# Router logits of a fused FFN kernel with the gate matrix as the stationary operand, in four column tiles

## Chip, cores, metric

One NeuronCore of a Trainium2 chip. The metric is the device time of one execution in microseconds; lower is better.

## What is computed

`x` is (64, 64, 512), 64 batches of 64 channels with 512 features. Each batch picks one of 8 conditioning matrices (64x64) and a bias; after that the 4096 rows of 512 features go through a mixture of 16 experts and one shared expert, and the result is added to `x`:

```python
h = einsum('bct,bcd->bdt', x, w[subjects]) + b[subjects][:, :, None]   # conditioning
h = h.reshape(4096, 512)
logits = h @ gate_weight.T                      # (4096, 16), the part that is changed
scores = sigmoid(logits)
biased = scores + expert_bias
# best 2 of 4 groups of experts by the sum of their top two, then the best 4 experts
w = scores[chosen]; w = w / w.sum() * 2.5
out = sum over the 4 chosen experts of w_e * down_e(silu(gate_e(h)) * up_e(h))
out = out + shared_down(silu(shared_gate(h)) * shared_up(h))
return x + out
```

All arrays are fp32.

## The kernel before

The rows are cut into 32 tiles of 128 (NT = 32). The kernel has a **first stage** (one loop over n = 0 to 33, written out), then the FFN of 32 tiles through the shared expert, then the FFN of 143 tiles of rows sorted by expert. Every engine has its own program; they meet by semaphores. Nothing plans the order but the order of the statements.

The first stage is a pipeline over the tiles. In iteration n

- **TensorE (PE)** multiplies tile n by its conditioning matrix (L770, `psY`, one fp32 product with 512 moving columns), transposes tile n-1 in four 128x128 blocks (L745, `psT`) and makes the logits of tile n-2 (L787, `psGU`): four products, one for each 128 features, with the transposed tile (128x128) stationary and the gate's 16 columns moving. It waits for tile n-2's evacuation before L770, for tile n-1's before the transposes, and for the copy of the transposed tile before the logits. An fp32 product shows as two weight loads and two matmuls in the trace, a transpose as one of each. After iterations 18 and 26 PE makes position sums for the routing (L755, L756; `PE_POS`).
- **ScalarE (ACT)** evacuates tile n with its bias to `tok_ring` (L625), copies the transposed tile n-1 to `kept_w` or, for the last eight, `x_ring` (L629), and takes the sigmoid of the logits of tile n-2 (L632). After iterations 16, 19 and 22 it also makes a third of the shared expert's split weights (L606).
- **GpSimd (POOL)** copies two 64x64 conditioning matrices into `cw_ring` for tile n (L537), up to eight tiles ahead of PE. After tile 4's it makes the late constants (`late_consts`, L493 and L501), after tile 10's it issues the DMAs that clear the padding rows.
- **SyncE (SP)** issues the load of tile n+8 when L770 has used tile n (L388), at n = 8 the load of the shared expert's weights (L395), and the store of tile n (L397). ACT waits for the store of tile n-8 before it overwrites its slot of `tok_ring`.
- **VectorE (DVE)** routes a batch of eight tiles when `scored` says that their sigmoids are there (`route_groups` and what follows). Batches 0 to 2 belong to this stage, and batch 1 is followed by three splits of shared weights (L1252). After batch 2 DVE makes the split of the first FFN tile (L1269), which PE's first FFN product waits for.

The FFN loop (PE L837, transposes L745) follows in the same programs. There PE carries in some iterations small products for the tables: L799 with a stationary operand of one column and 143 moving columns in fp32, L863 with 128x128 fp16 stationary and 144 moving.

Of the kernel before, what the change touches and what calls it, by code (L numbers as in the profile page):

```python
# [11 lines left out]
ACT = mybir.ActivationFunctionType  # L12
AX = mybir.AxisListType

P = 128
B, C, H = 64, 64, 512
N = B * C
NT = N // P
E, TOPK = 16, 4
# [3 lines left out]
HK, IK = H // P, I // P  # L23
UP = HK * 2 * I
EW = UP + IK * H
BC = 8
# [12 lines left out]
Q = P // QUADS  # L39
# [36 lines left out]
LOWS = {21: ((1, 0),), 23: ((1, 1),), 24: ((1, 2),), 26: ((2, 0),), 29: ((2, 1),), 31: ((2, 2),)}  # L76
RAW_LOADS = {14: 1, 15: 2, 23: 3, 31: 4}
WARM_UP = 12
X_COPIES = {1: 1, 5: 2, 9: 3, 13: 4, 17: 5, 21: 6, 25: 7}
FIRST_X_COPY = 30  # L80
WEIGHTS_STORE = 3
# [17 lines left out]

def tile_at(n):  # L100
    return Tile(n // RING, n % RING)


def run_tiles(eng, first, head, rounds, tail, step):
# [14 lines left out]
def build(nc, x, itok, fside, cond_w, gate_w, expert_bias, ffn_w, out):  # L119
# [4 lines left out]
    with ExitStack() as ctx:  # L124
        def sb(name, shape, dt=F32):
            return ctx.enter_context(nc.sbuf_tensor(name, shape, dt))

        def ps(name):
            return ctx.enter_context(nc.psum_tensor(name, [P, 512], F32))

        def sem(name):
            return ctx.enter_context(nc.semaphore(name))


        ident = sb("ident", [P, P])
# [14 lines left out]
        subj1h = sb("subj1h", [NS, B])  # L150
        fside2 = sb("fside2", [NS, 2 * C])
        bias_tok = sb("bias_tok", [P, NT])
        gate_sb = sb("gate_sb", [P, HK * E])
        ebias = sb("ebias", [P, E])
        raw_w = sb("raw_w", [P, 2 * EW])
        with nc.sbuf_tensor("kept_w", [P, SPLITS * 2 * EW], F32) as kept_w:
# [20 lines left out]
        scores = sb("scores", [P, NT * E])  # L177
# [93 lines left out]
        psY = [ps(f"psY{i}") for i in range(2)]  # L271
        psH = ps("psH")
        psM = ps("psM")


        consts = sem("consts")
# [23 lines left out]
        a_xposed = sem("a_xposed")  # L300
        a_xT_ready = sem("a_xT_ready")
        logits_done = sem("logits_done")
        scored = sem("scored")
        dve = sem("dve")
        cum_ready = sem("cum_ready")
# [57 lines left out]
        def kept_xT(tile):  # L363

            if tile >= NT - KEPT_IN_X:
                return x_ring[:, tile % RING, :]
            at = (1 + tile // KEPT) * 2 * EW + KEPT_ORDER[tile % KEPT] * H
            return kept_w[:, at:at + H]
# [220 lines left out]
        def _(act):  # L589
# [28 lines left out]
            for n in range(NT + 2):  # L618
                t = tile_at(n)
                if n < NT:  # L620
                    act.wait_ge(cond_done, n + 1)
                    if n >= RING:
                        act.wait_ge(h_stored[t.slot], t.rnd * 16)
                        act.wait_ge(a_xposed, n + 1 - RING)
                    act.activation(tok_ring[:, t.slot, 0:H], psY[n % 2][:], ACT.Identity,  # L625
                                   bias=bias_tok[:, n:n + 1]).then_inc(h_ready, 1)
                if 1 <= n <= NT:
                    act.wait_ge(a_xposed, n)
                    act.activation(kept_xT(n - 1), psT[(n + 1) % 2][:], ACT.Copy).then_inc(a_xT_ready, 1)  # L629
                if n >= 2:  # L630
                    act.wait_ge(logits_done, n - 1)
                    act.activation(scores[:, (n - 2) * E:(n - 1) * E], psGU[n % 2][:, 0:E],  # L632
                                   ACT.Sigmoid).then_inc(scored, 1)
                if n in SHARED_HIGH:
                    if SHARED_HIGH[n] == 0:
                        act.wait_ge(shared_loaded, 16)
                    split_high(0, SHARED_HIGH[n])
                elif n == FIRST_X_COPY:
                    copy_x(0)
                if n in (NT - 2, NT - 1):  # L640
                    copy_xT(tile_at(n - (NT - 2)), n - (NT - 2))
# [50 lines left out]
            def step(t, n, j):  # L692
# [19 lines left out]
                elif n in HIGHS:  # L712
# [4 lines left out]
                    split_high(turn, j)  # L717
                if n in X_COPIES:
                    copy_x(X_COPIES[n])

# [7 lines left out]
        def _(pe):  # L728
            pe.wait_ge(blank, 2)
            for _ in range(WARM_UP):  # L730
                pe.matmul(psM[:, 0:P], ones[:], ones[:], start=True, stop=True)  # L731
# [16 lines left out]
            def positions(b):  # L748
# [10 lines left out]
                    mm = pe.matmul(psM[:, BE:BE + E], ones[:], cum[:, NT, :], start=True, stop=True)  # L759
                mm.then_inc(pos_done, 1)  # L760

            for n in range(NT + 2):
                t = tile_at(n)
                if n < NT:

                    pe.wait_ge(x_in[t.slot], (t.rnd + 1) * 16)
                    pe.wait_ge(cond_w_ready, 2 * (n + 1))
                    if n >= 2:
                        pe.wait_ge(h_ready, n - 1)
                    pe.matmul(psY[n % 2][:], cw_ring[:, t.slot, :], x_ring[:, t.slot, :],  # L770
                              start=True, stop=True).then_inc(cond_done, 1)
                if n == 0:
                    bias()
                elif n == 2:
                    pe.wait_ge(small_loaded, SMALL)
                if 1 <= n <= NT:
                    pe.wait_ge(h_ready, n)
                    if n >= 3:
                        pe.wait_ge(a_xT_ready, n - 2)
                    transposes(psT[(n - 1) % 2], tok_ring[:, (n - 1) % RING, 0:H], HK).then_inc(a_xposed, 1)  # L780
                if n >= 2:
                    pe.wait_ge(a_xT_ready, n - 1)
                    if n >= 4:
                        pe.wait_ge(scored, n - 3)
                    xT = kept_xT(n - 2)
                    for k in range(HK):
                        mm = pe.matmul(psGU[n % 2][:, 0:E], xT[:, k * P:(k + 1) * P],  # L787
                                       gate_sb[:, k * E:(k + 1) * E], start=(k == 0), stop=(k == HK - 1))
                    mm.then_inc(logits_done, 1)
                if n in PE_POS:  # L790
                    positions(PE_POS[n])
# [73 lines left out]
                                   skip_group_check=True)  # L865
                mm.then_inc(table_done, 1)

            pe.wait_ge(scored, NT - 1)
            pe.wait_ge(h_ready, NT)
            pe.wait_ge(low_done, PIECES)  # L870
            kept = []
# [1 line left out]
            def step(t, n, j):  # L873
                if j == 0:
                    kept.clear()
                if n == NT:
                    pe.wait_ge(words_ready, 1)
                elif n == 1:
                    pe.wait_ge(scored, NT)
                at, needed = weights(t, n)  # L880
                kept.append(at)
                gate_up(t, n, kept[-1], needed)
                if n != 0:
                    xpose_hid(t + -1, None if n is None else n - 1)
                if n in PE_POS_FFN:
                    positions(PE_POS_FFN[n])
                elif n == PE_WORDS:
                    word_tables()
                elif n == PE_SP_WORDS:
                    sp_table()  # L890
                if is_shared(n):
                    for g in ENTRY_STEPS.get(n - 1, ()):
                        fill_slots(g)
                if n is None or n >= 2:
                    down(t + -2, None if n is None else n - 2,
                         kept[-3] if j >= 2 else weights(t + -2, None if n is None else n - 2)[0])
# [7 lines left out]
        def _(v):  # L904
# [43 lines left out]
            for half in range(2):  # L948
                a, b = half * C, half * C + C
# [16 lines left out]

            def route_groups(b):

                v.wait_ge(scored, (b + 1) * BC)
                tt(per_chunk(masked[:], E), per_chunk(batch(scores, b), E), over_chunks(ebias[:], BC), ALU.add)  # L970
                settle()
                four = masked[:].rearrange("p (g j) -> p g j", j=GS)
                tt(pair_sums[:, :, 0:3], four[:, :, 0:3], four[:, :, 1:4], ALU.add)
                tt(pair_sums[:, :, 3:5], four[:, :, 0:2], four[:, :, 2:4], ALU.add)
                tt(pair_sums[:, :, 5:6], four[:, :, 0:1], four[:, :, 3:4], ALU.add)
                settle()
                put(v.tensor_reduce(group_sum[:], pair_sums[:], AX.X, ALU.max))
                settle()

                sums = per_chunk(group_sum[:], NG)  # L980
                for d in range(1, NG):
                    last = d + (NG + 1) * (NG - 1 - d)
                    tt(beats[:, :, d:last + 1:NG + 1], sums[:, :, d:NG], sums[:, :, 0:NG - d], ALU.is_gt)
                settle()
                put(v.tensor_reduce(group_up[:], beats[:].rearrange("p c (a b) -> p c a b", b=NG), AX.X, ALU.add))
                put(v.tensor_reduce(group_down[:], beats[:].rearrange("p c (a b) -> p c b a", b=NG), AX.X, ALU.add))
                settle()
                tt(group_down[:], group_down[:], group_c[:], ALU.add)
                settle()
                tt(group_up[:], group_up[:], group_down[:], ALU.is_ge)  # L990
                settle()
                stt(four, spread(group_up[:].rearrange("p c g -> p (c g)"), GS), -BIG, four, ALU.mult, ALU.add)
                settle()
# [63 lines left out]
            used, not_last, start, end, turn, prep, prep_end = [e_rows[:, k, :] for k in range(7)]  # L1057
# [393 lines left out]
```

## Time and profile before

| | |
|---|---|
| median of 3 runs | 873.62 us (869.86 to 874.09) |
| the profiled execution's own time | 872.52 us |
| its span, first to last instruction | 870.8 us |
| PE busy | 851.7 us (98%) |
| DVE / ACT / POOL busy | 484.6 / 421.2 / 440.2 us |
| first stage, until the first L837 on the chain of waits | 79.74 us |

The span leaves 1.7 us of the profiled execution outside it. Times in the rows are microseconds from the span's start unless they are marked ns. PE is the matmul side of TensorE and PEld its weight loads; a matmul's duration includes its way through the array, so that matmuls one behind the other overlap in the timeline, and the chain of waits shows the time that each really adds. A line number can be that of a helper.

### The profile page before, as it was taken

What the parts mean: (1) busy time and instruction counts of PE and PEld (TensorE: products, weight loads), DVE (VectorE), ACT (ScalarE), POOL (GpSimd) and SP (SyncE); (2) the same over time, 40 slices, a digit from 0 to 9 for tenths busy, and PEclk for the clock granted to TensorE, in tenths of its full rate; (3) what the DMA queues carried; (4) which work ended last, traced back from release to release, by engine and by line L of the source; (5) the groups of instructions that cost most, each with busy time, mean ns of one, the idle gap of its engine ahead of it and who ended that gap; (6) DMA issues with size and microseconds to landing.
All of it is one profiled execution on the core that took longest, in us unless ns stands there. A gap on an engine that the chain in (4) does not pass through costs nothing.

```text
span 870.8 us, 19587 instructions
## 1 busy us (share of the span) xinstructions
PE 851.7 (98%) x4144; PEld 691.9 (79%) x4145; DVE 484.6 (56%) x1055; ACT 421.2 (48%) x884; POOL 440.2 (51%) x402
## 2 busy tenths in 40 slices
PE   9999999999999999999999999999999999999994
PEld 7778887878888888878888888888787878887883
DVE  1467786564654444664446645756557456464440
ACT  4675345754544444544445544645445455353441
POOL 4330211125547555656656666655655575755333
PEclk9999999999999999999999999999999999999998
DMA  8974576659999999999988999899798999989644
GB/s 258 352 277 145 114 128 164 165 110 291 258 219 270 195 183 188 176 221 281 209 179 172 234 260 226 176 269 229 193 280 178 284 243 234 244 179 194 123 62 62
DMA packets 147097, 179.10 MB, mean 206 GB/s; under 512 B 30986, under 2 KB 104210, under 8 KB 144658
## 3 DMA queue, kind: packets, MB, share of 16 engines
q0 software_dynamic: 37296, 86.95, 50.0%
q1 hardware_dynamic: 108258, 80.41, 35.1%
q10 hardware_dynamic: 1408, 10.49, 3.6%
q14 instruction: 117, 0.96, 0.4%
q8 instruction: 18, 0.29, 0.2%
HBM read 82.48 MB, written 65.04 MB: 169 GB/s over the span
## 4 chain that ended last, share of the span: by engine, by line
PE 85%; issue 4%; DVE 2%; ACT 2%; DMA 2%; SPq 1%; POOL 1%; DVEq 1%; ACTq 0%
PE psGU L837 48%; PE psY L837 24%; PE psH L745 4%; PE psY L770 3%; PE psGU L787 3%; DMA out<-y_ring,idx_all 2%; PE psT L745 2%; POOL out L553 1%; SPq L418 1%; ACT x_ring L689 1%; DVE entry L1244 1%; PE psM L731 1%; DVE x_ring L1246 1%; ACT y_ring L656 0%; ACT xT_hi L616 0%
## 5 line engine op out<-in xcount | busy, mean ns | idle before, releaser
L837 PE MATMUL psGU<-split_w,xT_hi 128*128 (+1 forms) x1400 | 432.6, 390 | 5.0 <-issue 2.7
L553 POOL DMA_INDIRECT out<-y_ring,idx_all x143 | 233.6, 1634 | 208.2 <-SPq L457 187.0
L837 PEld LDWEIGHTS psGU<-split_w,xT_hi 128*128 128x128 f32 x1400 | 261.9, 188 | 63.7 <-issue 8.1
L837 PE MATMUL psGU<-split_w,xT_lo 128*128 (+1 forms) x700 | 273.4, 391 | 0.0
L837 PE MATMUL psY<-split_w,hidT_hi 128*128 (+1 forms) x700 | 232.6, 413 | 0.2 <-issue 0.2
L704 ACT ACTIVATE aT<-psGU 128x256 f32<-128x256 f32 x175 | 67.2, 384 | 256.0 <-PE psGU L837 204.3
L1269 DVE TENSOR_TENSOR xT_lo<-psT,xT_hi 128x512 fp32r<-128x512 f32 x143 | 98.8, 691 | 150.6 <-ACT xT_hi L616 92.1
L548 POOL DMA_INDIRECT tok_ring<-h_rows,idx_all x143 | 150.2, 1051 | 57.6 <-issue 42.6
L656 ACT ACTIVATE y_ring<-psY 128x512 f32<-128x512 f32 x175 | 103.7, 593 | 127.3 <-PE psY L837 90.2
L837 PEld LDWEIGHTS psGU<-split_w,xT_lo 128*128 128x128 f32 x700 | 131.4, 188 | 27.4
L837 PE MATMUL psY<-split_w,hidT_lo 128*128 (+1 forms) x350 | 137.6, 393 | 0.0
L837 PEld LDWEIGHTS psY<-split_w,hidT_hi 128*128 128x128 f32 x700 | 118.5, 189 | 16.5 <-issue 0.7
L1294 DVE SCALAR_TENSOR_TENSOR aT<-aT,w_ring,psGU 128x256 f32<-128x256 f32 x143 | 66.9, 468 | 86.8 <-ACT aT L704 57.5
L1276 DVE STREAM_TRANSPOSE psT<-x_ring 128x512 f32<-128x512 f32 x143 | 102.5, 717 | 0.0
L561 POOL DMA_DIRECT2D out<-y_ring x32 | 28.4, 900 | 122.9 <-ACT y_ring L656 122.7
L616 ACT ACTIVATE xT_hi<-psT 128x512 fp32r<-128x512 f32 x143 | 84.7, 592 | 1.7 <-DVE psT L1276 1.2
L837 PEld LDWEIGHTS psY<-split_w,hidT_lo 128*128 128x128 f32 x350 | 65.7, 188 | 14.4
L1282 DVE TENSOR_TENSOR hidT_lo<-psH,hidT_hi 128x256 fp32r<-128x256 f32 x175 | 72.8, 416 | 2.1 <-ACT hidT_hi L647 1.3
L1309 DVE TENSOR_TENSOR split_w<-raw_w,split_w x42 | 51.5, 1226 | 39.1 <-ACT split_w L666 21.6
L647 ACT ACTIVATE hidT_hi<-psH 128x256 fp32r<-128x256 f32 x175 | 66.4, 380 | 3.0 <-PE psH L745 3.0
L745 PEld LDWEIGHTS psH<-ident,aT 128*128 128x128 f32 x350 | 48.7, 140 | 24.1 <-DVE aT L1292 1.3
L745 PE MATMUL psH<-ident,aT 128*128 128x128 f32 x350 | 66.6, 271 | 0.5 <-DVE hidT_lo L1282 0.5
(178 smaller groups left out, 495.7 us busy)
## 6 DMA issues: line engine op xcount, KB each, us to landing
x_ring<-tok_ring SPq DMA_DIRECT2D x284, 128.0 KB
raw_w<-ffn_w SPq DMA_DIRECT2D x17, 1536.0 KB, 10.4
h_rows<-tok_ring SPq DMA_DIRECT2D x32, 256.0 KB, 3.9
out<-y_ring POOLq DMA_DIRECT2D x32, 256.0 KB
x_ring<-x SPq DMA_DIRECT2D x24, 256.0 KB, 4.3
tok_ring<-h_rows,idx_all POOLq DMA_INDIRECT x143
out<-y_ring,idx_all POOLq DMA_INDIRECT x143
x_ring<-x ACTq DMA_DIRECT2D x8, 256.0 KB, 3.6
```

What stands on the lines that cost most here:

```text
L548: pool.indirect_dma_start(tok_ring[:, r % RING, :], None, h_rows[:, :], bass.IndirectOffsetOnAxis(idx_all[:, r:r + 1], 0)).then_inc(gather ...
L553: pool.indirect_dma_start(out[:, :], bass.IndirectOffsetOnAxis(idx_all[:, r:r + 1], 0), y_ring[:, r % YRING, :], None, compute_op=ALU.add) ...
L616: act.activation(xT_hi[:, t.slot % 2, :], xT, ACT.Copy).then_inc(xhi_ready, 1)
L647: act.activation(hidT_hi[:, t.slot % 2, :], psH[:, 0:I], ACT.Copy).then_inc(hidhi_ready, 1)
L656: act.activation(y_ring[:, s, :], psY[t.slot % 2][:], ACT.Copy).then_inc(y_ready, 1)
L704: act.activation(silu[:, t.slot % 2, :], psGU[t.slot % 2][:, 0:I], ACT.Silu).then_inc(silu_ready, 1)
L745: mm = pe.transpose(dst[:, k * P:(k + 1) * P], src[:, k * P:(k + 1) * P], ident[:])
L837: mm = pe.matmul(dst, a[:, slot, c], w(at + col + k * H), start=(k == 0 and a is high and at == 0), stop=(k == parts - 1 and a is low))
L1269: v.tensor_tensor(xT_lo[:, t.slot % 2, :], xT, xT_hi[:, t.slot % 2, :].bitcast(F32), ALU.subtract).then_inc(xT_ready, 1)
L1276: v.transpose(psT[t.slot % 2][:].rearrange("p (k b j) -> p k j b", k=HK, j=QUADS), x_duo[:, t.slot // DUO_TILES, :, t.slot % DUO_TILES, :] ...
L1282: v.tensor_tensor(hidT_lo[:, t.slot % 2, :], psH[:, 0:I], hidT_hi[:, t.slot % 2, :].bitcast(F32), ALU.subtract).then_inc(hidT_ready, 1)
L1294: ins = v.scalar_tensor_tensor(out=hid[:, half, :], in0=gate, scalar=w_ring[:, w_slot, bass.ds(expert, 1)], in1=up, op0=ALU.mult, op1=ALU. ...
```

## The change

The logits of tiles 0 to 27 are made in seven groups of four tiles. The gate matrix is padded from 16 to 32 columns and is now the stationary operand (128x32), the transposed tile (128x128) the moving one, and tile j of a group goes to the column tile j of TensorE (`tile_position=(0, j * Q)`), that is to partitions 32j to 32j+31 of `psLT`. That gives logits with the experts on partitions and the rows on the free axis. ACT copies the 128x128 block to SBUF (`logitsT`), PE turns it by one transpose (`psL`), and ACT takes one sigmoid of 128x64 for four tiles. Group g is made in iteration 4g+5 and turned in iteration 4g+6. Tiles 28 to 31 keep the former way, in iterations 30 to 33. Both PSUM blocks are columns 256 to 511 of `psH`. `scored` now counts 7 groups and then 4 tiles, and all who wait for it are changed to match.

```diff
@@ -76,6 +76,9 @@
 LOWS = {21: ((1, 0),), 23: ((1, 1),), 24: ((1, 2),), 26: ((2, 0),), 29: ((2, 1),), 31: ((2, 2),)}
 RAW_LOADS = {14: 1, 15: 2, 23: 3, 31: 4}
 WARM_UP = 12
+LOGIT_TILES = P // Q
+LOGIT_GROUPS = NT // LOGIT_TILES - 1
+DIRECT = LOGIT_GROUPS * LOGIT_TILES
 X_COPIES = {1: 1, 5: 2, 9: 3, 13: 4, 17: 5, 21: 6, 25: 7}
 FIRST_X_COPY = 30
 WEIGHTS_STORE = 3
@@ -99,6 +102,13 @@
 
 def tile_at(n):
     return Tile(n // RING, n % RING)
+
+
+def scored_by(tiles):
+
+    if tiles <= DIRECT:
+        return tiles // LOGIT_TILES
+    return LOGIT_GROUPS + tiles - DIRECT
 
 
 def run_tiles(eng, first, head, rounds, tail, step):
@@ -150,7 +160,8 @@
         subj1h = sb("subj1h", [NS, B])
         fside2 = sb("fside2", [NS, 2 * C])
         bias_tok = sb("bias_tok", [P, NT])
-        gate_sb = sb("gate_sb", [P, HK * E])
+        gate_sb = sb("gate_sb", [P, HK * Q])
+        logitsT = sb("logitsT", [P, P])
         ebias = sb("ebias", [P, E])
         raw_w = sb("raw_w", [P, 2 * EW])
         with nc.sbuf_tensor("kept_w", [P, SPLITS * 2 * EW], F32) as kept_w:
@@ -271,6 +282,7 @@
         psY = [ps(f"psY{i}") for i in range(2)]
         psH = ps("psH")
         psM = ps("psM")
+        psLT, psL = psH[:, 2 * P:3 * P], psH[:, 3 * P:4 * P]
 
 
         consts = sem("consts")
@@ -300,6 +312,8 @@
         a_xposed = sem("a_xposed")
         a_xT_ready = sem("a_xT_ready")
         logits_done = sem("logits_done")
+        logitsT_ready = sem("logitsT_ready")
+        logits_turned = sem("logits_turned")
         scored = sem("scored")
         dve = sem("dve")
         cum_ready = sem("cum_ready")
@@ -627,8 +641,17 @@
                 if 1 <= n <= NT:
                     act.wait_ge(a_xposed, n)
                     act.activation(kept_xT(n - 1), psT[(n + 1) % 2][:], ACT.Copy).then_inc(a_xT_ready, 1)
-                if n >= 2:
-                    act.wait_ge(logits_done, n - 1)
+                g, phase = divmod(n - LOGIT_TILES, LOGIT_TILES)
+                if 0 <= g < LOGIT_GROUPS and phase == 1:
+                    act.wait_ge(logits_done, g + 1)
+                    act.activation(logitsT[:], psLT, ACT.Copy).then_inc(logitsT_ready, 1)
+                elif 0 <= g < LOGIT_GROUPS and phase == 2:
+                    act.wait_ge(logits_turned, g + 1)
+                    act.activation(scores[:, g * LOGIT_TILES * E:(g + 1) * LOGIT_TILES * E].rearrange(
+                        "p (j e) -> p j e", e=E), psL.rearrange("p (j q) -> p j q", q=Q)[:, :, 0:E],
+                        ACT.Sigmoid).then_inc(scored, 1)
+                if n - 2 >= DIRECT:
+                    act.wait_ge(logits_done, scored_by(n - 1))
                     act.activation(scores[:, (n - 2) * E:(n - 1) * E], psGU[n % 2][:, 0:E],
                                    ACT.Sigmoid).then_inc(scored, 1)
                 if n in SHARED_HIGH:
@@ -759,6 +782,25 @@
                     mm = pe.matmul(psM[:, BE:BE + E], ones[:], cum[:, NT, :], start=True, stop=True)
                 mm.then_inc(pos_done, 1)
 
+            def group_logits(g):
+
+                pe.wait_ge(a_xT_ready, (g + 1) * LOGIT_TILES)
+                if g > 0:
+                    pe.wait_ge(logitsT_ready, g)
+                for k in range(HK):
+                    for j in range(LOGIT_TILES):
+                        mm = pe.matmul(psLT[j * Q:(j + 1) * Q, :], gate_sb[:, k * Q:(k + 1) * Q],
+                                       kept_xT(g * LOGIT_TILES + j)[:, k * P:(k + 1) * P],
+                                       start=(k == 0), stop=(k == HK - 1), tile_position=(0, j * Q))
+                mm.then_inc(logits_done, 1)
+
+            def turn_logits(g):
+
+                pe.wait_ge(logitsT_ready, g + 1)
+                if g > 0:
+                    pe.wait_ge(scored, g)
+                pe.transpose(psL, logitsT[:], ident[:]).then_inc(logits_turned, 1)
+
             for n in range(NT + 2):
                 t = tile_at(n)
                 if n < NT:
@@ -778,14 +820,19 @@
                     if n >= 3:
                         pe.wait_ge(a_xT_ready, n - 2)
                     transposes(psT[(n - 1) % 2], tok_ring[:, (n - 1) % RING, 0:H], HK).then_inc(a_xposed, 1)
-                if n >= 2:
+                g, phase = divmod(n - LOGIT_TILES, LOGIT_TILES)
+                if 0 <= g < LOGIT_GROUPS and phase == 1:
+                    group_logits(g)
+                elif 0 <= g < LOGIT_GROUPS and phase == 2:
+                    turn_logits(g)
+                if n - 2 >= DIRECT:
                     pe.wait_ge(a_xT_ready, n - 1)
-                    if n >= 4:
-                        pe.wait_ge(scored, n - 3)
+                    if n - 4 >= DIRECT:
+                        pe.wait_ge(scored, scored_by(n - 3))
                     xT = kept_xT(n - 2)
                     for k in range(HK):
                         mm = pe.matmul(psGU[n % 2][:, 0:E], xT[:, k * P:(k + 1) * P],
-                                       gate_sb[:, k * E:(k + 1) * E], start=(k == 0), stop=(k == HK - 1))
+                                       gate_sb[:, k * Q:k * Q + E], start=(k == 0), stop=(k == HK - 1))
                     mm.then_inc(logits_done, 1)
                 if n in PE_POS:
                     positions(PE_POS[n])
@@ -865,7 +912,7 @@
                                    skip_group_check=True)
                 mm.then_inc(table_done, 1)
 
-            pe.wait_ge(scored, NT - 1)
+            pe.wait_ge(scored, scored_by(NT - 1))
             pe.wait_ge(h_ready, NT)
             pe.wait_ge(low_done, PIECES)
             kept = []
@@ -876,7 +923,7 @@
                 if n == NT:
                     pe.wait_ge(words_ready, 1)
                 elif n == 1:
-                    pe.wait_ge(scored, NT)
+                    pe.wait_ge(scored, scored_by(NT))
                 at, needed = weights(t, n)
                 kept.append(at)
                 gate_up(t, n, kept[-1], needed)
@@ -966,7 +1013,7 @@
 
             def route_groups(b):
 
-                v.wait_ge(scored, (b + 1) * BC)
+                v.wait_ge(scored, scored_by((b + 1) * BC))
                 tt(per_chunk(masked[:], E), per_chunk(batch(scores, b), E), over_chunks(ebias[:], BC), ALU.add)
                 settle()
                 four = masked[:].rearrange("p (g j) -> p g j", j=GS)
@@ -1436,7 +1483,8 @@
         "itok": np.ascontiguousarray(itok_B_0_7),
         "fside": np.tile(np.asarray(fside_8xS_0), (1, 2)),
         "cond_w": np.tile(np.asarray(L0_cond_weights).transpose(1, 0, 2).reshape(C, NS * C), (2, 1)),
-        "gate_w": np.ascontiguousarray(columns(np.asarray(L0_ffn_gate_weight)[None])[0].reshape(P, HK * E)),
+        "gate_w": np.ascontiguousarray(np.pad(columns(np.asarray(L0_ffn_gate_weight)[None])[0],
+                                              ((0, 0), (0, 0), (0, Q - E))).reshape(P, HK * Q)),
         "expert_bias": np.ascontiguousarray(L0_ffn_expert_bias),
         "ffn_w": np.ascontiguousarray(ffn_w),
     }
```

## Rows read from the trace of the kernel before

**Rows 1.** The page: the chain that ended last, by engine and by line

```profile
PE 85%; issue 4%; DVE 2%; ACT 2%; DMA 2%; SPq 1%; POOL 1%; DVEq 1%; ACTq 0%
PE psGU L837 48%; PE psY L837 24%; PE psH L745 4%; PE psY L770 3%; PE psGU L787 3%; DMA out<-y_ring,idx_all 2%; PE psT L745 2%; POOL out L553 1%; SPq L418 1%; ACT x_ring L689 1%; DVE entry L1244 1%; PE psM L731 1%; DVE x_ring L1246 1%; ACT 
```

**Rows 2.** Windows of the first stage: PE, PEld, DVE, ACT, POOL busy (x), clock, DMA share, GB/s

```profile
40.00:60.00 20.00, 20.00 (x131) 15.39 (x130) 12.76 (x46) 14.71 (x30) 9.09 (x28) 1.00 0.93 327
60.00:80.00 20.00, 19.99 (x137) 15.99 (x136) 10.44 (x46) 12.65 (x30) 0.04 (x1) 1.00 0.46 164
```

**Rows 3.** The chain in order of time, first stage: start us, us, what

```profile
16.41 0.72 issue
17.13 1.10 PE psY L770 x2
...
39.18 0.95 PE psY L770 x2
40.13 0.44 PE psT L745 x4
40.57 0.80 PE psGU L787 x8
...
47.95 0.32 PE psM L755 x2
48.26 0.22 PE psM L756 x2
48.48 0.86 PE psY L770 x2
...
79.74 5.57 PE psGU L837 x24
```

**Rows 4.** Groups of PE and PEld instructions, 0 to 86 us, shapes apart

```profile
L787 PE MATMUL psGU<-gate_sb,kept_w 128*128 128x16 f32 x192 | 23.1, 253 | 0.0
L787 PEld LDWEIGHTS psGU<-gate_sb,kept_w 128*128 128x128 f32 x192 | 23.3, 192 | 0.0
```

**Rows 5.** The chain in order of time, two stretches of the FFN: start us, us, what

```profile
124.47 0.52 PE psM L863 x8
...
138.61 2.08 PE psT L799 x18
```

**Rows 6.** Timeline of ACT in iteration 16: start, us

```profile
42.36 0.69 ACT L625 ACTIVATE tok_ring<-psY,bias_tok 128x512 f32<-128x512 f32 x1 [0.77 <-PE psY L770]
42.95 0.59 ACT L629 ACTIVATE kept_w<-psT 128x512 f32<-128x512 f32 x1
43.60 0.18 ACT L632 ACTIVATE scores<-psGU 128x16 f32<-128x16 f32 x1
43.68 1.05 ACT L606 ACTIVATE split_w<-raw_w 128x1024 fp32r<-128x1024 f32 x1
```

**Rows 7.** Timeline of POOL: start, us; the copies for tiles 5, 16 and 17

```profile
16.51 0.52 POOL L537 COPY cw_ring<-cond_sb 64x64 f32 x2 [1.90 <-issue]
...
35.62 0.57 POOL L537 COPY cw_ring<-cond_sb 64x64 f32 x2 [2.42 <-issue]
38.75 0.53 POOL L537 COPY cw_ring<-cond_sb 64x64 f32 x2 [2.57 <-PE psY L770]
```

**Rows 8.** DMA: windows of 2 us, columns as in rows 2

```profile
42.00:44.00 2.00, 2.00 (x15) 1.60 (x14) 0.00 (x0) 1.57 (x4) 0.46 (x2) 1.00 1.06 403
...
54.00:56.00 2.00, 2.00 (x15) 1.47 (x14) 1.76 (x8) 1.17 (x4) 1.04 (x4) 1.00 0.77 210
```

**Rows 9.** DMA: issue to landing of the loads of x at L388

```profile
DMA to landing us min/median/max: 2.6/4.3/12.3
```

**Rows 10.** Timeline of DVE: routing of batch 2 and the first FFN tile's split

```profile
63.98 0.29 DVE L920 TENSOR_TENSOR masked<-scores,ebias 128x128 f32<-128x128 f32 x1 [4.32 <-ACT scores L632]
...
73.69 0.23 DVE L1049 TENSOR_SCALAR weights_te<-w_num 128x128 f32<-128x128 f32 x1
76.52 0.69 DVE L1269 TENSOR_TENSOR xT_lo<-x_ring,xT_hi 128x512 fp32r<-128x512 f32 x1 [2.60 <-ACT xT_hi L616]
```

## The prediction

> **What bounds the kernel now.** I read the page's chain first: PE's work makes 85% of it, and the lines of the first stage stand in it, L770 with 3% and the logits, L787, with 3% [rows 1]. Windows of that stage show PE busy throughout at a granted clock of 1.00, its full level (2.4 GHz), ACT, the nearest other engine, at 14.7 of 20 us at most, but the DMA engines at a share of 0.93 from 40 to 60 us [rows 2]. The chain in order of time shows one iteration: 0.95 us for the conditioning product, 0.44 for four transposes, 0.80 for the logits, 2.19 together, nothing between them [rows 3]. So time taken from PE in this stage shortens the kernel until another wait comes up; the nearest are looked at below. The logits' 256 weight loads and matmuls (192 of each in the first form) stream 16 columns, and a pair adds 0.80/8 = 0.10 us though the matmul lasts 253 ns and the load 192 [rows 3, 4]: they pay for loading 128 columns.
>
> One stretch gives nothing. In iteration 5 PE waits 0.72 us until 17.13 us for the conditioning matrix of tile 5 [rows 3], which POOL copies only at 16.51, behind the late constants [rows 7]. The logits of tiles 0 to 2 lie ahead of that; without them PE only waits longer.
>
> **The change, part by part.**
>
> *Removed:* the logits of tiles 3 to 27, which lie behind 17.13 us: 25 x 0.80 = 20.0 us [rows 3].
>
> *A weight load uncovered before, covered after:* L770 adds 0.95 us behind logits but 0.86 behind the position sums, which stream 128 columns [rows 3]. Of the 26 iterations 6 to 31, seven stay behind a group, one behind direct logits and two were behind position sums already, so 16 x 0.09 = 1.4 us go.
>
> *Added, seven groups of logits.* A group is 16 fp32 products (four blocks of features, four tiles), each two passes: 32 loads and 32 matmuls of 128 fp32 moving columns. Such a pass costs 0.44/4 = 0.11 us in the transposes [rows 3], and with a small stationary operand 2.08/18 = 0.116 for 143 columns [rows 5], by columns 0.104; I take 0.107. Whether passes in different columns of the array overlap, no row shows. The bounds are 32 x 0.107 = 3.4 us, one behind the other, and 8 x 0.107 = 0.86, all four column tiles at once. I take the middle: the code issues both passes of a product together, and both need the same column tile, so the second has to follow the first; if PE starts matmuls in program order, only the second pass of one product runs beside the first of the next. That is 16 x 0.107 = 1.71 us. The issue of instructions allows it: eight fp16 pairs add 0.52 us, 0.065 a pair [rows 5], and 32 x 0.065 = 2.1 is thus an upper bound for issue alone.
>
> "TensorEngine Tiling (Array Packing)" of the Trainium skill (Theoretical Speedup) gives up to 4x for 32 columns; by it a group would be 0.86 us. "TensorE: Matmul & The Clock Gate" of the Trainium skill (Part 3) says that matmuls start and end in program order; by it 1.71 stands. No row here decides between them.
>
> *Into and out of the column tiles:* if the array must empty first, each change costs what a matmul outlasts its addition, 0.253 - 0.10 = 0.15 us [rows 3, 4]; if not, nothing. I take the whole, 0.32 us a group with the two rounded up, since the other end is only hoped for. (The Trainium skill, "TensorEngine Tiling (Array Packing)", Key Properties, says that a change of tiling mode drains TensorE.)
>
> *Seven transposes:* 0.11 us each. Together 7 x (1.71 + 0.32 + 0.11) = 15.0 us.
>
> *ACT.* An iteration takes it 0.59 + 0.65 = 1.24 us (starts 42.36, 42.95, 43.60) [rows 6] against 0.86 + 0.44 = 1.30 on PE in those without a group. Per four tiles, four sigmoids of 0.18 give way to a copy of 128 columns and a sigmoid of 64; their cost lies between 0.18 and 0.59 each by the same rows, some 0.5 us together. The 1.05 us of L606 [rows 6] had 0.95 us of slack each iteration (2.19 - 1.24); now after iterations 19 and 22 a transpose waits for the late evacuation, about 0.5 us each; after 16 the group of iteration 17 covers it. I add 1.0 us. The waits for the copy and the turned block have an iteration of other work between them, and what is queued behind them on ACT, the next tile's evacuation, isn't due before; nothing for them.
>
> *POOL, DMA, DVE.* Four tiles then take 4 x 1.30 + 0.09 + 2.14 = 7.4 us. Tile 17's product comes at 17.13 + 3 x 7.4 = 39.4 us, where POOL's copy for it, not held by PE for all that row's name says (tile 9 had passed), ends at 39.3 [rows 7]: just enough. The load of x for eight tiles later has 14.9 - 0.9 = 14.0 us, and landing took at most 12.3 [rows 9]. The DMA engines moved 403 GB/s while saturated and 210 by 54 us when a backlog (shared weights, cleared padding) was gone [rows 8]; 0.52 MB for each 1.86 us is 282 GB/s, so the backlog still drains, later. The gate's 32 KB more go nowhere near a wait. Batch 2's routing takes from 63.98 to 73.92 us, 9.9 us, and the FFN begins 15.8 us after its start [rows 3, 10]; after, its scores come in iteration 26, some 13 us ahead of the FFN. The first split then starts in time. Nothing for all of these. The FFN behind starts earlier with all its work and passes the gain on.
>
> **Sum:** -20.0 - 1.4 + 15.0 + 1.0 = -5.4 us. The profiled execution took 872.5 us and would take 867.1; it lies 1.1 us under the median, so the median goes from 873.6 to **868.2 us**.
>
> **The rivals.**
>
> *All four column tiles at once* (chance 0.21). For it: loads and matmuls of one product already overlap [rows 4]. Then 7 x (0.86 + 0.32 + 0.11) = 9.0 us and a sum of -11.4. But tile 17 would be due at 17.13 + 12 x 1.30 + 0.27 + 3 x 1.29 = 36.9 us, 2.4 us before POOL has it [rows 7], and the lead of a load of x falls to 12.3 us, what the longest needed [rows 9]. So -9.0: 864.6 us.
>
> *No overlap, and TensorE loses* (0.22). The 32 passes stand one behind the other: 7 x (3.42 + 0.32 + 0.11) = 27.0 us against 21.4 taken away, ACT's stalls gone with the slower pace: +5.6, 879.2 us. It decides from 2.63 us a group upward, (21.4/7) less 0.43. For it: no row shows two matmuls side by side at more than the array's rate; against: a column tile leaves three quarters of the array free.
>
> *The gain is taken by the next wait* (0.12): the pairs overlap, but POOL's 2.5 us gaps [rows 7], which came at a DMA share of 1, grow with a longer backlog, or the splits of ACT hold more than I count. Three to five us go: about 872 us.
>
> The forecast has the remaining 0.45, its own range -4 to -7.5 us by the drain paid or not.
>
> **How the numbers follow.** About 0.5%, 4.4 us, is what a measurement of this kernel can tell from no change. The forecast lies just beyond it, two thirds of its chance above: 0.31 faster, 0.14 same. Full overlap is faster. No overlap is slower by more than that if the drain is paid (0.15), else same (0.07). The third rival is same. Faster 0.52, same 0.33, slower 0.15. The range from 862.5 to 878.5 takes in full overlap with part of POOL's wait and cuts off the worse half of no overlap.
>
> **What would show it.** The chain of waits would have seven pieces of 32 matmuls on `psH`; by the forecast each adds 1.7 to 2.1 us, by full overlap about 1.0, by none 3.4 or more. L770 would add 0.86 us in most iterations. The first FFN product would start at 74.3 us in place of 79.74. ACT would have gaps behind PE of about half a microsecond near its splits, POOL none that PE waits for after tile 5. The forecast is wrong if the groups' pieces are near either end, if PE waits for POOL or a load of x in iterations 12 to 20, or if an earlier start of the FFN isn't seen at the end. A granted clock under 1.00 in the stage would upset every term.

## The result, and the profile after

The changed kernel took **864.07 us** (median of 6 runs, 861.59 to 866.22) against 873.48 us (6 runs, 869.86 to 875.10) for the kernel before: a ratio of 0.989, 95% interval 0.9868 to 0.9913, so 9.4 us less. Run again beside other kernels it took 864.10 us against 872.34, ratio 0.9913 (0.9884 to 0.9942). The forecast was 868.2 us, 5.4 less, in a range of 862.5 to 878.5.

| profiled execution | before | after |
|---|---|---|
| its own time | 872.52 us | 861.59 us |
| span | 870.8 us | 859.8 us |
| PE busy | 851.7 us | 838.1 us |
| first stage, until the first FFN product on the chain | 79.74 us | 72.25 us |
| the rest of the span | 791.1 us | 787.5 us |

The chain that ended last in the changed kernel, by line; it answers to [rows 1] (L884 is L837 of before, L812 is L770, L834 the direct logits of L787, L792 the new groups):

```profile
PE psGU L884 52%; PE psY L884 26%; PE psH L768 4%; PE psY L812 3%; PE psT L768 1%; DMA x_ring<-x 1%; PE psH L792 1%; ACT x_ring L712 1%; DVE entry L1291 1%; DVE x_ring L1293 1%; POOL out L567 1%; ACT split_w L620 0%; PE psGU L834 0%; ACT xT
```

The logits' 3% are gone down to 1% for L792 and less for L834, and a new piece stands there, a load of x. The chain in order of time, in the changed kernel, which answers to [rows 3] (start us, us, what):

```profile
13.94 3.66 issue
17.60 2.05 PE psY L812 x2
19.65 0.85 PE psT L768 x4
20.50 1.87 PE psH L792 x32
22.37 1.73 PE psY L812 x2
...
28.54 1.01 PE psH L792 x32
29.55 1.05 PE psY L812 x2
...
31.04 0.11 PE psH L802
...
32.05 9.33 DMA x_ring<-x
...
41.43 1.12 PE psY L812 x2
...
49.70 0.66 PE psT L768 x4
...
72.25 5.60 PE psGU L884 x24
```

A group of 32 matmuls adds **1.01 us** (28.54), which is full overlap and not pairs. Its turning transpose adds 0.11 (31.04). The product behind a group adds 1.05 us, 0.19 over the 0.86 of a covered load. But the first group adds 1.87 us, and the pieces beside it are long too: PE waited 3.66 us for tile 5's matrix (13.94), and after that its clock was at half. The windows of 2 us show it (PE, PEld, DVE, ACT, POOL busy (x), granted clock, DMA share, GB/s):

```profile
14.00:16.00 2.00, 0.00 (x0) 0.00 (x0) 0.00 (x0) 0.71 (x2) 0.85 (x1) 1.00 1.04 383
16.00:18.00 2.00, 0.40 (x1) 0.43 (x2) 0.00 (x0) 0.00 (x0) 0.47 (x2) 0.72 0.82 309
18.00:20.00 2.00, 2.00 (x5) 0.86 (x5) 0.00 (x0) 0.31 (x1) 0.93 (x4) 0.50 0.10 37
...
22.00:24.00 2.00, 2.00 (x11) 0.80 (x4) 0.00 (x0) 0.28 (x1) 1.33 (x3) 0.58 0.17 56
24.00:26.00 2.00, 2.00 (x13) 1.44 (x12) 0.00 (x0) 1.75 (x4) 2.00 (x4) 1.00 0.75 192
```

No matmul ran from 14 to 16 us; from 16 to 24 us the granted clock falls to 0.50, the lower of its two levels (1.2 GHz), and back to 1.00 (2.4 GHz) in the window from 24. The four pieces from 17.60 us take 2.05 + 0.85 + 1.87 + 1.73 = 6.50 us; at the full level, by the same chain and [rows 3], they are 1.10 + 0.44 + 1.01 + 1.05 = 3.60. So in this trace the wait, of which 0.72 us was there before [rows 3], costs 2.9 us more through the clock.

Who kept PE waiting in the stage, changed kernel, 10 to 74 us (us in total, times, longest us):

```profile
PE psY L812 <- issue: 3.7, 1, 3.7
PE psY L812 <- DMA x_ring<-x: 1.2, 1, 1.2
PE psT L768 <- ACT tok_ring L639: 0.4, 2, 0.2
```

The first line is the wait for POOL's copies for tile 5, which began at 16.98 us and took 0.52, the second the load of x for tile 17, in iteration 17 (texts below that were written before a run call it iteration 13, a miscount of mine), the third ACT held by the splits. Per load of x, issue to landing went from a median of 4.3 us to 7.8, at a longest of 10.4 (12.3 before, [rows 9]):

```profile
DMA to landing us min/median/max: 2.5/7.8/10.4
```

The load that PE waits for took 9.3 us on the chain, from its issue at 32.05 us. Tile 9's product, which frees its slot, had ended at 28.1 us. SP's timeline around it (start us, us):

```profile
27.80 1.24 SPq L402 DMA_DIRECT2D x_ring<-x  x1
29.09 1.55 SPq L409 DMA_DIRECT2D raw_w<-ffn_w  x1
30.68 1.33 SPq L411 DMA_DIRECT2D h_rows<-tok_ring  x1
32.05 0.89 SPq L402 DMA_DIRECT2D x_ring<-x  x1
```

The issues of tile 16's load, of the shared weights and of a store stand ahead of it in SP's program and take 1.24, 1.55 and 1.33 us, at a DMA share of 1.0. So the load was asked for 4.0 us after its slot was free, took 9.3 us more, and was needed sooner than before, since the iterations were shorter.

### The profile page after: what moved, and what is told of

The parts are those of the page before. It is cut to its first block, busy times and chain, and to the rows that moved or that the text cites. A ratio compares the mean times of both kernels' runs of the same rounds, so it can differ in the third digit from the quotient of the medians.

```text
span 859.8 us, 19571 instructions
## 1 busy us (share of the span) xinstructions
PE 838.1 (97%) x4151; PEld 675.4 (79%) x4152; DVE 485.0 (56%) x1055; ACT 418.1 (49%) x870; POOL 439.2 (51%) x402
## 4 chain that ended last, share of the span: by engine, by line
PE 89%; issue 3%; ACT 3%; DVE 2%; DMA 1%; POOL 1%; DVEq 0%; ACTq 0%; SPq 0%
PE psGU L884 52%; PE psY L884 26%; PE psH L768 4%; PE psY L812 3%; PE psT L768 1%; DMA x_ring<-x 1%; PE psH L792 1%; ACT x_ring L712 1%; DVE entry L1291 1%; DVE x_ring L1293 1%; POOL out L567 1%; ACT split_w L620 0%; PE psGU L834 0%; ACT xT_hi L630 0%; PE psM L910 0%
## 5 line engine op out<-in xcount | busy, mean ns | idle before, releaser
L884 PE MATMUL psGU<-split_w,xT_hi 128*128 (+1 forms) x1400 | 432.0, 390 | 3.0 <-DVE xT_lo L1316 3.0
L884 PEld LDWEIGHTS psGU<-split_w,xT_hi 128*128 128x128 f32 x1400 | 262.2, 188 | 60.2 <-issue 4.2
L884 PE MATMUL psGU<-split_w,xT_lo 128*128 (+1 forms) x700 | 273.4, 391 | 0.0
L884 PE MATMUL psY<-split_w,hidT_hi 128*128 (+1 forms) x700 | 232.5, 413 | 0.2 <-issue 0.2
L562 POOL DMA_INDIRECT tok_ring<-h_rows,idx_all x143 | 148.2, 1037 | 61.0 <-issue 42.7
L884 PEld LDWEIGHTS psGU<-split_w,xT_lo 128*128 128x128 f32 x700 | 131.4, 188 | 27.4
L884 PE MATMUL psY<-split_w,hidT_lo 128*128 (+1 forms) x350 | 137.5, 393 | 0.0
L884 PEld LDWEIGHTS psY<-split_w,hidT_hi 128*128 128x128 f32 x700 | 118.5, 189 | 16.1 <-issue 0.5
L884 PEld LDWEIGHTS psY<-split_w,hidT_lo 128*128 128x128 f32 x350 | 65.7, 188 | 14.4
```

Of the source, the lines that this page charges most:

```text
L562: pool.indirect_dma_start(tok_ring[:, r % RING, :], None, h_rows[:, :], bass.IndirectOffsetOnAxis(idx_all[:, r:r + 1], 0)).then_inc(gather ...
L884: mm = pe.matmul(dst, a[:, slot, c], w(at + col + k * H), start=(k == 0 and a is high and at == 0), stop=(k == parts - 1 and a is low))
```

## Experiments

**Is it four column tiles side by side, or cheap passes?** Two runs. `j_outer` exchanges the loops of a group, so that eight passes in one column tile follow one another:

```diff
-                for k in range(HK):
-                    for j in range(LOGIT_TILES):
+                for j in range(LOGIT_TILES):
+                    for k in range(HK):
```

> The changed kernel with the two loops of a group exchanged, so that the eight passes of one tile, all in one column tile, stand one behind the other. Theory A (column tiles work side by side, passes in the same column tile one behind the other): a group's piece on the chain goes from 1.01 us to 3.4 us (32 x 0.107), or a little less where the last pass of one tile overlaps the first of the next, and the FFN starts 7 x 2.3 = 16 us later. Rival B (a narrow stationary operand alone makes a pass of 128 columns cost 0.03 us, wherever it goes): the piece stays at 1.0 us and the start of the FFN stays within 1 us.

`one_tile` leaves out three of four tiles' logits in groups 1 to 6:

```diff
-                    for j in range(LOGIT_TILES):
+                    for j in range(LOGIT_TILES if g == 0 else 1):
```

> The changed kernel with groups 1 to 6 making the logits of their first tile only (8 of 32 passes; the logits of the other three tiles are left over from group 0). Theory A (four column tiles fully side by side): the eight passes in one column tile take as long as the 32 in four, 8 x 0.107 = 0.86 us and 0.15 on the way in, so a group's piece stays at 1.01 us. Rival B (each pass costs 0.03 us wherever it goes): 0.25 to 0.4 us a piece. Forecast on record (pairs of passes side by side) would have had 0.86 against 1.71.

The chains in order of time, first `j_outer`, then `one_tile`:

```profile
26.67 2.39 PE psH L792 x32
```

```profile
28.08 0.99 PE psH L792 x8
```

Eight passes in one column tile take 0.99 us, as long as the 32 in four (1.01): the column tiles run fully side by side, and rival B is out (it wanted 0.4 at most). With the loops exchanged the same 32 passes take 2.39 us, so the order matters; but it is 2.39 and not 3.4. The FFN accordingly starts 5.3 us later than in the changed kernel (77.53 against 72.25 us; 71.58 in `one_tile`) and not 16: the groups add 7 x 1.38 = 9.7 us, and the half clock (2.9) and the wait for x (1.5 with the longer piece behind it) are absent from this trace. How many matmuls are in flight shows why. Windows of 0.05 us over a group, L792 alone (x counts the matmuls and loads that run in the window), changed kernel:

```profile
28.45:28.50 0.05, 0.03 (x4) 0.04 (x6) 1.00 0.50 205
28.55:28.60 0.05, 0.05 (x5) 0.05 (x8) 1.00 0.64 248
28.60:28.65 0.05, 0.05 (x8) 0.05 (x8) 1.00 0.34 123
28.70:28.75 0.05, 0.05 (x12) 0.05 (x8) 1.00 1.26 497
28.75:28.80 0.05, 0.05 (x12) 0.05 (x4) 1.00 1.06 412
```

The same for `one_tile`, and then for `j_outer`:

```profile
28.35:28.40 0.05, 0.05 (x3) 0.05 (x2) 1.00 1.02 410
```

```profile
26.95:27.00 0.05, 0.05 (x3) 0.05 (x1) 1.00 1.03 420
27.05:27.10 0.05, 0.05 (x4) 0.05 (x4) 1.00 0.95 376
27.30:27.35 0.05, 0.05 (x6) 0.05 (x3) 1.00 0.45 164
28.00:28.05 0.05, 0.05 (x6) 0.05 (x3) 1.00 1.31 532
```

One column tile has 3 matmuls in flight, each 0.27 us long and 0.11 apart. The changed kernel has 12, four times as many: four start in the first 0.05 us, the next four 0.13 us after the first, and the others at steps of 0.11. In `j_outer` there are 3 at first and then 5 or 6, two column tiles' worth: the second tile's first passes start 0.46 us into the group, when not more than five of the first tile's eight have started. Starts in strict program order would have held them back until 0.75 us and given 3 x 0.75 + 0.99 = 3.2 us in all. So by these figures PE looks past matmuls that wait for their column tile, but not far enough for more than two tiles at eight passes each; the order that spreads neighbours over the tiles gets all four. When the next tile begins in `j_outer`, three passes of the tile before it are still waiting; in the changed kernel the fourth tile's first pass would go past three waiting second passes, if the instructions stand as in the code. One reach, of three waiting matmuls, would fit both orders; no run tried it. (The Trainium skill, "TensorE: Matmul & The Clock Gate", Part 3, says that matmuls start and end in program order; `j_outer` does not agree, unless the passes of different products stand in another order in the instructions than in the code, which no view here shows.) `j_outer` lasted 871.28 us in its one run, 871.16 the median of before; one run can't show the 2.2 us by which its FFN starts ahead of 79.74.

**What do the wait for POOL and the half clock cost?** `kept_warm` fills the wait with work that leaves its result unused:

```diff
+                elif n == 4:
+                    for _ in range(WARM_UP + 4):
+                        pe.matmul(psM[:, 0:P], ones[:], ones[:], start=True, stop=True)
```

> The changed kernel with 16 more fp32 products of ones with ones, 128 columns, on PE at the end of iteration 4, in the time in which it waits for the conditioning matrix of tile 5 (32 passes x 0.107 = 3.4 us of a wait of 3.66). Theory: the granted clock stays at 1.00, the product of tile 5 still starts at about 17.6 us, but the pieces of iterations 5 and 6 that took 2.05, 0.85, 1.87 and 1.73 us take 1.1, 0.44, 1.0 and 1.05, so that the FFN starts 2.9 us earlier (69.3 us instead of 72.25) unless the wait for a load of x in iteration 13, 1.2 us, grows by as much. Rival (PE only runs into the loads of x sooner, the lost clock costs nothing): the wait in iterations 12 to 15 grows to about 4 us and the FFN starts at 71.5 to 72.3. Total 861 by the theory, 864 by the rival.

The clock stayed at 1.00 throughout the stage; `kept_warm`, windows of 2 us:

```profile
16.00:18.00 2.00, 2.00 (x15) 1.64 (x15) 0.00 (x0) 0.53 (x1) 0.70 (x3) 1.00 0.62 240
18.00:20.00 2.00, 2.00 (x39) 1.36 (x37) 0.00 (x0) 1.29 (x4) 0.92 (x4) 1.00 0.33 68
20.00:22.00 2.00, 2.00 (x9) 1.13 (x9) 0.00 (x0) 1.25 (x3) 0.87 (x5) 1.00 0.59 220
```

The first two groups added 1.01 us each. But the FFN started at 71.05 us, 1.2 earlier and not 2.9: between the theory's 69.3 and the rival's 71.5. In `kept_warm` PE waits for a load of x until 40.22 us, 1.75 us, and before that for POOL in iterations 12 and 13:

```profile
29.48 1.10 PE L812 MATMUL psY<-x_ring,cw_ring 128*128 128x512 f32 x2 [0.19 <-issue]
31.62 1.10 PE L812 MATMUL psY<-x_ring,cw_ring 128*128 128x512 f32 x2 [0.60 <-issue]
40.22 1.12 PE L812 MATMUL psY<-x_ring,cw_ring 128*128 128x512 f32 x2 [1.75 <-DMA x_ring<-x]
```

Both accounts are half right: the clock's 2.9 us are real, and POOL and the loads take 1.7 of them back. The total, 865.98 us against 871.16 (ratio 0.9933, 0.9904 to 0.9962), does not show even the 1.2; it is above the 861 and 864 us that were expected, and the measurement does not tell it from the changed kernel's 0.989.

`tables8` moves the cause of the wait, POOL's late constants, behind tile 8 (`PAIR_TABLES = 8` for 4):

> The changed kernel with POOL's late constants behind the copies for tile 8 instead of tile 4. Theory: PE does not wait for POOL after tile 4 and the clock stays up; the 3.66 us of waiting and 2.9 us of half clock go, unless DMA takes them back: the loads of x for tiles 8 to 15 are asked for earlier, but the DMA engines are at a share of about 1. With all of it the FFN starts at 65.7 us; I expect 2 to 3 us of waits for loads of x to stay or come, so 67 to 69 us and a total of 859 to 861. Rival (DMA is what sets the pace of the stage after tile 8): the start stays above 71 us.

The FFN started at 71.65 us: the rival's side. The wait was only moved, to tile 9, and took the clock with it (1.6 us by the pieces behind it); and shorter ones for POOL came up behind it, 2.3 us together. `tables8`, chain in order of time:

```profile
20.55 2.41 issue
22.95 1.11 PE psY L812 x2
...
24.92 1.87 PE psH L792 x32
...
31.70 0.96 issue
...
38.63 0.81 issue
```

So the time behind tile 8 was POOL's and the DMA engines' to give, and the next runs go there. (Total 860.99 us against 871.16, ratio 0.9864, 0.982 to 0.9908: as low as expected, though the start of the FFN was not.)

**Who holds POOL's copies and the loads of x?** `pads31` issues the four DMAs that clear the padding rows, 2.1 MB, after tile 31 (`PAD_STORES = 31` for 10):

> The changed kernel with the four DMAs that clear the padding rows issued by POOL after tile 31's copies instead of tile 10's. In the traces so far POOL's copies for a tile come 1.0 to 1.3 us apart before those DMAs and about 2 us apart for some eight tiles behind them, and the wait for tile 13's load of x ends at 41 us, when the DMA engines have been at a share of 1 for 14 us. Theory (these DMAs hold up both): the copies stay 1.0 to 1.3 us apart, the 1.2 us wait for x in iteration 13 goes, and the FFN starts at 70.5 to 71.0 us, with the half clock of iterations 5 and 6 still there. Rival (the shared weights and the tiles' own traffic saturate the DMA engines): the wait for x stays over 0.8 us and the start within 0.4 us of 72.25.

The wait for x went, and the FFN started at 70.48 us, at the lower edge of the theory's, with the half clock still there. The longest landing of a load of x fell to 9.2 us:

```profile
DMA to landing us min/median/max: 2.5/6.7/9.2
```

The issue of tile 17's load came 1.0 us after tile 9's product had ended (27.8 us) and not 4.0, because the issues ahead of it on SP took 0.43 us each:

```profile
28.78 0.43 SPq L402 DMA_DIRECT2D x_ring<-x  x1
```

POOL's copies stayed 1.0 to 1.7 us apart until 34 us, but then went to 1.2 to 2.4 without those DMAs, when the DMA engines were still at a share of 1. So in this one trace the wait for x went with the padding, which explains only the first part of POOL's slow copies; what slows the rest was not settled. Total 861.54 us against 872.19, ratio 0.9872 (0.983 to 0.9915).

`t12_p31` adds `PAIR_TABLES = 12`:

> As pads31, and POOL's late constants behind the copies for tile 12 instead of tile 4. Theory: PE waits for POOL nowhere, the clock stays at 1.00, all of the 3.66 + 2.9 + 1.4 us of waits and half clock goes: FFN start at 64.5 to 66 us, total 6 to 7 us under the changed kernel. Rival (waits for loads of x take at least half of it back, since eight tiles of x are in flight and now asked for earlier): start at 68 to 70 us.

FFN start at 66.49 us, just behind the theory's window: the half clock of the stage is gone, of the waits for POOL one of 1.68 us is left, now in iteration 13, and one of 0.3. `t12_p31`, chain in order of time:

```profile
26.72 1.68 issue
...
35.41 0.29 issue
```

The total, 860.49 us (ratio 0.9847, 0.9797 to 0.9898), is 3.6 us under the changed kernel's and not 6 to 7: the part behind the stage took 793.1 us, 5.6 more than in the changed kernel's trace. Of these the last section has a reason for 1.6.

`t12_p31_splits` adds the move of ACT's split pieces:

```diff
-SHARED_HIGH = {16: 0, 19: 1, 22: 2}
+SHARED_HIGH = {17: 0, 21: 1, 25: 2}
```

> As t12_p31, and ACT's three pieces of the shared weights' split after iterations 17, 21 and 25, in which PE has a group, instead of 16, 19 and 22. Theory: PE's two waits for an evacuation held up by them, 0.5 us each, go; FFN start 1.0 us before that of t12_p31. Rival (ACT is then late for the group's copy and the next evacuation): no difference within 0.3 us, the waits only move.

FFN start at 65.29 us, 1.2 earlier. The product of tile 18, which stands ahead of the waits behind the splits, already started 0.4 us earlier, with 1.4 us of waits for POOL in place of 2.0; the other 0.8 are the two waits for ACT. The chain has no piece of ACT between 15 and 64 us any more. The theory holds: a split in an iteration with a group costs nothing. The totals, 860.49 and 859.86 us, don't tell the two apart.

`before_t12_p31` makes the same two moves on POOL in the kernel before:

> The kernel before with the same two moves on POOL (late constants behind tile 12, clearing DMAs behind tile 31). Theory: there only the wait of 0.72 us for tile 5's matrix exists, so the FFN starts at 79.0 us instead of 79.74 and the total is the same within what can be measured. If the total falls by more than 2 us, the moves are worth something by themselves and not only with the change.

FFN start at 78.71 us, 870.0 us against 872.19, ratio 0.9975 (0.9948 to 1.0003). The moves are worth one microsecond of stage there, 5.8 in the changed kernel (72.25 to 66.49), by one trace of each; two traces of the changed kernel differ by 1.1 (below). Before, other work of PE covered most of what they take away: PE waited once, for 0.72 us, and not at all in `before_t12_p31`.

**All together.** `combined` is `t12_p31_splits` with the two fp16 tables of the late constants also made after tile 31 (DVE's wait for them moves to where it uses them), and `after_again` the changed kernel beside it:

```diff
+            def fp16_consts():
                 iota(lane_q[:], [[1, P], [0, DUO]], 0, 0)
...
                 elif n == PAD_STORES:
                     clear_pads()
+                    pool.wait_ge(cond_w_ready, 2 * (n + 1))
+                    fp16_consts()
```

> As t12_p31_splits, and the two fp16 tables, 3.2 us of the late constants, made by POOL after tile 31 with the clearing DMAs; the other constants stay behind tile 12. Theory: the last wait of PE for POOL, 1.36 us in iteration 13, goes: FFN start at 63.5 to 64.2 us, 1.3 us before t12_p31_splits, and the total 4 to 6 us under after_again. Rival (POOL's slow copies, not the constants, make that wait, or a load of x takes its place): start at 65 us or later.

> The changed kernel itself, unaltered, beside the next run on the same chip: it gives what its FFN start and its FFN part vary by. FFN start again at 71.5 to 73 us with half clock after tile 5's wait; the rest of the span between 787 and 793 us, as in the ten traces so far.

`combined` took **854.52 us** (853.22 to 862.03) against 864.10 for `after_again` and 872.34 for the kernel before; its ratio to the latter is 0.981 (0.9775 to 0.9845), apart from the changed kernel's 0.9884 to 0.9942. Its FFN starts at 63.30 us, a bit ahead of the theory's window, and the total is 9.6 us under `after_again`, more than the 4 to 6 expected. The profile lists no wait of PE in the stage, while for `after_again` it lists these (10 to 74 us):

```profile
PE psY L812 <- issue: 3.2, 1, 3.2
PE psY L812 <- DMA x_ring<-x: 2.5, 1, 2.5
```

The DMA engines of `combined` are busier than before [rows 2], and PE waits for nobody (windows as above):

```profile
20.00:40.00 20.00, 20.00 (x177) 12.56 (x176) 10.47 (x50) 16.15 (x32) 8.18 (x34) 1.00 1.02 364
40.00:60.00 20.00, 20.00 (x184) 13.09 (x182) 18.53 (x77) 16.56 (x33) 11.96 (x21) 1.00 0.96 349
```

`after_again` started its FFN at 73.34 us, a microsecond beyond the changed kernel's first trace (outside what I expected by 0.3), with a wait for x of 2.5 us instead of 1.2, after which the clock was at half a second time.

## Why the prediction came out as it did

The total lay in the range and on the forecast side, but that is in part luck. The step that carried the sum failed: the seven groups cost 8.5 us and not 15.0, and costs that the sum did not have (the half clock 2.9, a load of x 1.5, tile 5's later matrix 0.5) took 4.9 of the difference back. By the signs that it named itself it was wrong: the groups' pieces lie at the end that full overlap gave, PE waited for a load of x in iteration 17, and the granted clock fell under 1.00. The stage gave 7.5 us in the first trace (6.4 in `after_again`), the medians of the total 9.4 (8.2); where the rest comes from was not settled.

- *What bounds it:* right. Time taken from PE in the stage shortened the kernel. Over the twelve traces, with FFN starts from 63.3 to 79.7 us, the rest of the span was 787.4 to 793.5 us. The three earliest starts have 793.0 to 793.5, for 1.6 us of which the last section has a reason in two of them; but `kept_warm`, with a start at 71.05, has 792.8 too, so whether an early start costs the FFN something was not settled. Of the first trace's 11.0 us, 7.5 are the stage's, and the other 3.5 lie within that spread.
- *Tiles 0 to 2 give nothing:* right, and worse. The 0.72 us wait grew to 3.66, as was said; that such a wait can take the clock down was not said. It cost 2.9 us in the first trace, and `kept_warm` shows that work in the wait keeps the clock up.
- *The group, 1.71 us, by pairs of passes:* **this step failed**. It is 1.01 us, 0.86 for eight times four passes side by side and 0.15 on the way in. The forecast's premise, that the second pass of a product holds up the next product, is refuted by the 12 matmuls in flight, with four starts in 0.05 us; it would have been nearer in `j_outer`, where 2.39 us were measured. The rival with all four tiles at once (chance 0.21) had the mechanism, and by it 864.6 us, half a microsecond from the measured 864.1, but not by its own reason: it took 2.4 us off for POOL's copy of tile 17, and what came off was the clock and a load of x. Its stage sum was -9.0 against -7.5, so that its total came so near is luck too.
- *Into and out of the column tiles, 0.32 us:* it measured 0.15 on the way in and 0.19 on the product behind, 0.34, where 0.09 of the latter was counted in the line before. The size is right. The drain that the Trainium skill ("TensorEngine Tiling (Array Packing)", Key Properties) states fits these rows, though they don't tell it from a weight load that can't be made ahead.
- *A covered load of L770 saves 0.09:* right, 0.86 us in every iteration without a group before it, outside the waits.
- *ACT, 1.0 us:* right. The two waits behind the splits cost 0.42 us each (0.20 of idleness and 0.22 of a longer piece of transposes, 0.66 in place of 0.44), 0.8 together, and `t12_p31_splits` takes them away.
- *POOL just enough, DMA lead 14.0 us:* POOL was in time after tile 5, since the half clock had given it 2.9 us. The lead of a load was not: four iterations took 6.5 us and not 7.4, which leaves 13.0 - 0.9 = 12.1 us, and 4 of them went by before SP issued the load. That cost 1.2 us of wait and 0.26 of a longer piece. The forecast counted the time to landing and not the time to issue.

With the measured terms the sum is -20.0 - 1.4 + 7 x (1.01 + 0.10 + 0.11) + 2.9 (clock) + 1.5 (x) + 0.8 (ACT) + 0.5 (tile 5's matrix came that much later) - 0.2 (the two position sums add 0.22 us behind a transpose and added 0.32 behind logits) = -7.4 us, against -7.5 on the chain.

## To carry to other kernels

Small products with a stationary side of 32 columns are worth putting in column tiles, if the loop changes the tile with every product: the same 32 passes took 1.01 us so and 2.39 in the other order. The swap of the operands alone would have gained nothing: by `one_tile` four tiles in one column tile are estimated at 4 x 0.86 = 3.4 us, against 4 x 0.80 = 3.2 for the direct logits. When work is taken from PE ahead of a wait, look at what the wait does to the clock: 3.66 us of idleness cost another 2.9, and such a fall cost between 1.5 and 2.8 in other traces. And a faster stage should be read again for work of other engines that was free before: two moves on POOL took 1.0 us from the old kernel's stage and 5.8 from the new one's, and with two more the new kernel went from 864.1 to 854.5 us. The kernel before with all four moves was not run.

## What the hardware showed unexpectedly

- Matmuls in different column tiles overlap fully in fp32, 12 in flight against 3 in one tile, and the overlap depends on how near the tiles' products stand in the program (1.01 against 2.39 us for the same 32 passes).
- The granted clock was at half after waits of PE of 3.66 us (changed kernel), 3.72 (`pads31`), 3.53 (`one_tile`), 2.41 (`tables8`), 3.22 and 2.5 (both `after_again`), and stayed at 1.00 after waits of 3.39 (`j_outer`), 1.68 (`t12_p31`) and 1.75 (`kept_warm`): the length alone does not decide. Nor is the price fixed: the four pieces from the wait's end took 2.9 us more than at the full level in the changed kernel and 1.5 in `after_again` (2.05 + 0.85 + 1.15 + 1.05 against 3.60).
- It fell once more without a wait: in five of the twelve traces the first 24 matmuls of the FFN added 6.9 to 7.2 us instead of 5.6, right behind the last transposes and direct logits, on a PE that was busy throughout. `pads31`, windows of 5 us:

```profile
65.00:70.00 5.00, 4.99 (x41) 4.33 (x39) 4.59 (x16) 4.00 (x11) 0.00 (x0) 1.00 0.91 295
70.00:75.00 5.00, 5.00 (x19) 4.01 (x19) 2.85 (x14) 1.72 (x4) 0.00 (x0) 0.66 0.18 52
```

What separates the traces with this drop from those without was not tried.
